# Freeing two kinds of PSUM bank earlier in the slot, and one matmul group moved by a slot, in a cross-attention and FFN kernel

## The chip, the cores and the metric

The kernel runs on one core of one Trainium2 chip. The metric is the device time of one execution in microseconds (us). A core has a matrix engine (PE; its weight loads are shown as PEld), a vector engine (DVE), an activation engine (ACT), a general engine (POOL) and a queue that starts transfers (SP). Each works through its own list of instructions in order, and they wait for each other with counting semaphores. PE writes only to PSUM, which has eight banks of 128x512 float32.

## The reference

```
x = x + attention(layernorm(x), ctx, mask)     # x 2x2048x512, ctx 2x128x512, 16 heads of 32
    q = layernorm(x) @ wq + bq ; k, v = ctx @ wk + bk, ctx @ wv + bv
    score = q k^T / sqrt(32) * mask ; where(score == 0, -1e9, score) ; softmax over the 128 keys
    out   = (softmax @ v) @ wo + bo
x = x + (real(ifft(fft(layernorm(x)) @ w_complex)) + bias)
```
The second part is linear, so the kernel folds the two Fourier transforms and the complex weights into one 512x512 matrix M in its first sixth, and then multiplies by M.

## The kernel before

The 4096 rows are cut into 16 chunks of 256 (chunk c). The heads of a chunk are worked in four groups of four, so there are 64 score tiles s = 4c + g (128 x 1024 scores each: two tiles of 128 rows, four heads, 128 keys). The main loop runs over slots v = 2 to 79; a chunk's worth of work is four slots, v = 4c + r with r = 0 to 3, and the stages are staggered over the slots:

- PE, slot v: every second slot (r even) the softmax-times-V product PV, from `weigh`; the transposes of score tile v-2 (`turn`, L606); one "mid" product (r = 0, 1: output projection WO of chunk c-2, half 0 or 1; r = 2, 3: FFN product FF of chunk c-3); the scores of tile v+1 (`scores`, L594); then the "late" products.
- DVE, slot v: scores times mask (`mask_mul`, L890), in odd slots the division of the context by the softmax sum (`ctx_norm`, L914), the replacement of zeros (`zero_to_neg`, L897), the row minimum (`least`, L902), then `lo(n)` for the held and the mid products, then layernorm statistics (`stats1`, `stats2`, L928, L971) and the reciprocal of the sums (`recip`, L908).
- ACT, slot v: in odd slots `copy_rec` (L725), four exponentials of tile v-1, two copies of transposed scores (L718), four more exponentials (L709), in odd slots `ctx_hi` (L732), then `hi(n)` for the held and the mid products, casts for the layernorms.
- POOL: the scale of the minimum into a bias for the exponentials (`bias`, L1124), low halves of split operands, bias additions, `spread` (L1131), which prepares R, and `stat_cols`, which prepares ST.

All products other than scores, transposes and PV are called fills and are numbered n in the order of PE's list. They share three PSUM banks: fill n goes to bank n mod 3 and may start only when fill n-3 is free. The kinds that matter are: QQ, a pair of query projections (24 matmuls, L454); R, the reciprocals turned by four transposes (L555); ST, the rows of layernorm statistics (two matmuls in `stat_rows`, L462); U and M, pieces of the folding of the FFN matrix; WO and FF (12 matmuls each, L449).

```
if n >= 3:
    pe.wait_ge(g_free, n - 2)
```
A bank is freed by DVE at the end of `lo(n)`, in the order of n. For QQ, DVE itself subtracts (L862) after ACT has made the high half (L683). For ST, ACT copies the rows (`stat_copy`, L649), and for R, ACT copies the bank in `copy_rec` (L725); DVE then only issues an empty instruction (L847) that adds one to `g_free`:

```
elif kind in ("ST", "R"):
    dve.engine_nop().then_inc(g_free, 1)
    return
```
Late fills of slot v are "held": their `hi` and `lo` run in slot v+1, behind `least` on DVE and behind the second four exponentials and `ctx_hi` on ACT. Mid fills are handled in their own slot. Before, the steady order of the fills is r0: WO, R, ST; r1: WO, QQ; r2: FF, R; r3: FF, QQ. That is nine fills for three banks, so each stands three places behind the same one in every chunk: QQ of r1 behind R of r0, FF of r2 behind ST, WO of r1 behind WO of r0.

Chunk c's queries and statistics go to their stacked form through 14 transfers on SP (`stack_q`, at slot 4c-5), of which the last two (`stack_rows`) wait for ST's copy.

Of the kernel before, what the change touches and what calls it, by code (L numbers as in the profile page):

```python
# [17 lines left out]
NC = NB * S // CH  # L18
# [18 lines left out]
def plan():  # L37

    fills, slots, held = [], {}, []
    lead = [("W1", 0), ("CT", 0), ("CT", 1), ("K", 0), ("ST", 0), ("Q", 0, 0), ("Q", 0, 1), ("S", 0),
            ("W1", 1), ("Q", 0, 2), ("S", 1), ("K", 1), ("Q", 0, 3), ("ST", 1), ("Q", 1, 0), ("S", 2),
            ("Q", 1, 1), ("Q", 1, 2), ("Q", 1, 3)]
    front = []
    for f in lead:
        if f[0] == "S":
            front += [("S", f[1], 0), ("S", f[1], 1)]  # L50
        else:
            front.append(("G", len(fills)))
            fills.append(f)
    early = {
# [3 lines left out]
    }  # L58
    queries = {2: (2, 0), 4: (2, 1), 5: (3, 0), 6: (3, 1)}
    for v in range(V0, V1):  # L60
        c, r = divmod(v, 4)
        mid = {
            0: [("WO", c - 2, 0)],
            1: [("WO", c - 2, 1)],
            2: [("FF", c - 3, 0)],
            3: [("FF", c - 3, 1)],
        }[r]
        mid = [f for f in mid if 0 <= f[1] < NC] + early.get(v, [])
        if mid == [LAST]:
            mid = [LAST, (*LAST, "right")]  # L70
        late = []
        if v % 2 == 0 and 0 <= v - 4 < NS:
            late.append(("R", (v - 4) // 2))
        if v % 4 == 0 and 3 <= v // 4 + 2 < NC:
            late.append(("ST", v // 4 + 2))
        if v in queries:
            late.append(("QQ",) + queries[v])
        elif v >= 7 and v % 2 == 1 and (v + 9) // 4 < NC:
            late.append(("QQ", (v + 9) // 4, (v + 9) % 4 // 2))
        base = len(fills)  # L80
        fills += mid + late
        mids = list(range(base, base + len(mid)))
        lates = list(range(base + len(mid), len(fills)))
        items = []
        if v % 2 == 0 and 0 <= v - 4 < NS:
            items += [("PV", (v - 4) // 2)]
        if 0 <= v - 2 < NS:
            items += [("PT", v - 2, 0), ("PT", v - 2, 1)]
        items += [("G", n) for n in mids]
        if 0 <= v + 1 < NS:  # L90
            items += [("S", v + 1, 0), ("S", v + 1, 1)]
        items += [("G", n) for n in lates]
        slots[v] = (items, held, mids)
        held = lates
    return fills, front, slots


def stats_slot(c, t):
# [7 lines left out]
def hi_slot(c):  # L106
    return 5 if c == 4 else 4 * (c - 3)
# [11 lines left out]
def build(nc, x, xt, ctx_in, mask, wq, bq, wk, bk, wv, bv, wo, bo, lparts, tables, bf, eye, sums, pick, places, heads, out):  # L119
    fills, front, slots = plan()  # L120
    at = {f: n for n, f in enumerate(fills)}

    with ExitStack() as stack:
# [519 lines left out]
        def _(act):  # L643
# [42 lines left out]
            def high_m(c):  # L686
                act.wait_ge(g_free, at["M", c] + 1)
                act.activation(mh[:, c, :], mf[:], ACT.Identity, scale=SO / D).then_inc(m_hi, 1)

            def split_hi(c):  # L690
                act.wait_ge(d_xt[c % NT], 16 * (c // NT + 1))
                if c >= 2:
                    act.wait_ge(g_done, last_query(c - 2) + 1)
                act.copy(xth[:, c % 2], xtr[:, c % NT]).then_inc(h1_done, 1)
# [8 lines left out]
            def exps(s, t):  # L703
                if t == 0:
                    act.wait_ge(p_nb, s + 1)
                for j in range(4):
                    z = zs[:, s % NZ, t, j, :]
                    i = 4 * t + j
                    last = act.activation(z, z, ACT.Exp, bias=nbias[:, s % 4, i:i + 1], scale=-NEG,  # L709
                                          accum_out=zsum[:, s % 4, i:i + 1])  # L710
                if t == 1:
                    last.then_inc(ex_done, 1)

            def copy_pt(s, f):
                act.wait_ge(pt_done, 2 * s + f + 1)
                if f == 0 and s >= 2:
                    act.wait_ge(pv_done, s // 2)
                act.copy(pt[:, s % 2, 2 * f:2 * f + 2, :], PB[f][:]).then_inc(pt_copied, 1)  # L718

            def copy_rec(m):  # L720
                n = at["R", m]
                act.wait_ge(g_done, n + 1)
                if m >= 1:
                    act.wait_ge(cn_done, m)
                act.copy(rec[:], G[n % 3][:].rearrange("p (i n) -> p i n", i=2)).then_inc(rc_done, 1)  # L725

            def ctx_hi(m):
                c, h = divmod(m, 2)
                act.wait_ge(cn_done, m + 1)
                if h == 0 and c >= 2:  # L730
                    act.wait_ge(g_done, at["WO", c - 2, 1] + 1)
                act.copy(ch[:, c % 2, 2 * h:2 * h + 2, :], cn[:]).then_inc(ch_done, 1)  # L732
# [37 lines left out]
            hi(at["Q", 1, 3])  # L770
            for v in range(V0, V1):
                c, r = divmod(v, 4)
                held, mids = slots[v][1:]
                if v % 2 == 1 and 0 <= v - 5 < NS:
                    copy_rec((v - 5) // 2)
                if 2 <= v - 1 < NS:
                    exps(v - 1, 0)
                if 0 <= v - 2 < NS:
                    copy_pt(v - 2, 0)
                    copy_pt(v - 2, 1)  # L780
                if v == 2:
                    act.wait_ge(d_wo, 16)
                    act.activation(wos[:], wos[:], ACT.Identity, scale=SO).then_inc(w_sc, 1)
                    act.wait_ge(w_sc, 1)
                    act.copy(woh[:], wos[:]).then_inc(w_hi, 1)
                if 2 <= v - 1 < NS:
                    exps(v - 1, 1)
                if v % 2 == 1 and 0 <= v - 5 < NS:
                    ctx_hi((v - 5) // 2)
                if 0 <= v - 9 < 4:  # L790
                    high_m(v - 9)
                for n in held:
                    hi(n)
                if v == 3:
                    split_hi(3)
                for n in mids:
                    hi(n)
                if r == 1 and 0 <= c - 2 < NC:
                    norm_hi2(c - 2, 0)
                if r == 2 and 0 <= c - 2 < NC:  # L800
                    norm_hi2(c - 2, 1)
                for a in range(4, NC):
                    if hi_slot(a) == v:
                        split_hi(a)
        @block.vector
        def _(dve):
# [103 lines left out]
            def ctx_norm(m):  # L910
                dve.wait_ge(rc_done, m + 1)
                if m >= 1:
                    dve.wait_ge(p_cl, m)
                dve.tensor_tensor(cn[:], CX[:].rearrange("p (i n) -> p i n", i=2), rec[:], ALU.mult).then_inc(cn_done, 1)  # L914
# [100 lines left out]
            lo(at["Q", 1, 3])  # L1015
            for v in range(V0, V1):
                c, r = divmod(v, 4)
                held, mids = slots[v][1:]
                if 0 <= v < NS:
                    mask_mul(v)  # L1020
                if v % 2 == 1 and 0 <= v - 5 < NS:
                    ctx_norm((v - 5) // 2)
                if 0 <= v < NS:
                    zero_to_neg(v)
                if 0 <= v < NS:
                    least(v)
                if 0 <= v - 9 < 4:
                    low_m(v - 9)
                for n in held + mids:
                    lo(n)  # L1030
                tasks = []
                tasks += [(stats1, mean1, a, t) for a in range(4, NC) for t in range(2) if stats_slot(a, t) == v]
                if r == 0 and 0 <= c - 2 < NC:
                    tasks.append((stats2, mean2, c - 2, 0))
                if r == 1 and 0 <= c - 2 < NC:
                    tasks.append((stats2, mean2, c - 2, 1))
                for stats, _, *ct in tasks:
                    stats(*ct)
                if v % 2 == 1 and 0 <= v - 3 < NS:
                    recip((v - 3) // 2)  # L1040
                for _, mean, *ct in tasks:
                    mean(*ct)
                if c - 2 == NC - 1 and r < 2:
                    last_lo2(r)
                if v in (4, 5):
                    for n in range(3 * v - 6, 3 * v - 3):
                        fold(n)
# [312 lines left out]
```

## Time and profile before

| | |
|---|---|
| median of three runs | 487.33 us (487.2 to 487.72) |
| profiled execution | 487.75 us, of which the span of its instructions is 486.0 us |
| PE busy | 441.3 us (91%) |
| DVE busy | 403.6 us (83%) |
| ACT busy | 366.8 us (75%) |
| POOL busy | 349.3 us (72%) |
| mean granted clock of PE | 0.993 of full speed |

Busy time says how long instructions of an engine were under way. Where two engines are both near the span, what matters is at which points one stands idle, and what ended that idle time. "DVEq" as a releaser is DVE's sequencer, here the empty instruction of L847.

### The profile page before, as it was taken

How to read it: one execution, taken by the hardware profiler on the slowest of the kernel's cores; microseconds unless marked ns; L12 is line 12 of the kernel's file. 1: busy time of each engine (PE TensorE's matmuls, PEld its weight loads, DVE VectorE, ACT ScalarE, POOL GpSimd, SP SyncE). 2: the span in 40 equal slices, each digit the busy share in tenths (PEclk: the TensorE clock that was granted, in tenths of full speed). 3: DMA queues.
4: the chain of work that ended last, by engine and by line, in shares of the span. 5: the costliest groups of instructions: out<-in, count | busy, mean ns of one | idle time of the engine just before them, and what ended most of it. 6: DMA issues, size and time to landing. Idle time of an engine off the chain costs nothing.

```text
span 486.0 us, 10923 instructions
## 1 busy us (share of the span) xinstructions
PE 441.3 (91%) x3510; PEld 298.5 (61%) x3510; DVE 403.6 (83%) x538; ACT 366.8 (75%) x1342; POOL 349.3 (72%) x476
## 2 busy tenths in 40 slices
PE   7989859968889898989898999989898989989897
PEld 5777647747566565656565656666565665655444
DVE  3797589867989898898989898989899888999543
ACT  3358757757978888878979888888888879989810
POOL 6579552853867969696969697887969776865663
PEclk9999999979999999999999999999999999999999
DMA  8995834223415355454445353535442333321334
GB/s 285 394 349 142 289 110 107 66 59 86 90 48 143 101 142 113 129 128 117 108 128 118 85 128 103 146 99 141 104 101 70 93 75 83 76 58 30 88 98 120
DMA packets 85286, 60.15 MB, mean 124 GB/s; under 512 B 40141, under 2 KB 72813, under 8 KB 84718
## 3 DMA queue, kind: packets, MB, share of 16 engines
q1 hardware_dynamic: 84508, 59.29, 45.5%
q8 instruction: 29, 0.48, 0.4%
q10 hardware_dynamic: 722, 0.17, 0.2%
q14 instruction: 27, 0.22, 0.1%
HBM read 29.33 MB, written 8.39 MB: 78 GB/s over the span
## 4 chain that ended last, share of the span: by engine, by line
PE 49%; DVE 24%; ACT 10%; issue 10%; DMA 3%; SPq 2%; POOL 1%; DVEq 0%; ACTq 0%; POOLq 0%
PE bank L454 16%; PE bank L449 16%; DVE zs L897 7%; ACT zs L709 6%; PE bank L606 6%; PE bank L620 5%; DVE nmin L902 4%; DVE zs L890 3%; DVE cn L914 2%; PE scores L594 2%; ACT pt L718 2%; DVE st L971 2%; DVE x L869 2%; SPq L287 2%; DMA cxs<-in_ctx 2%
## 5 line engine op out<-in xcount | busy, mean ns | idle before, releaser
L709 ACT ACTIVATE zs<-zs,nbias 128x128 f32<-128x128 f32 x512 | 199.5, 395 | 18.6 <-POOL nbias L1124 18.3
L718 ACT COPY pt<-bank 128x512 f32<-128x512 f32 x128 | 67.9, 581 | 41.5 <-PE bank L606 41.5
L709 ACT ACTIVATION_READ_ACCUMULATOR zs<-zs,nbias 128x1 f32 x512 | 98.5, 192 | 0.0
L897 DVE SCALAR_TENSOR_TENSOR zs<-zs 128x1024 f32<-128x1024 f32 x64 | 88.7, 1386 | 1.2
L902 DVE TENSOR_REDUCE nmin<-zs 128x8 f32<-128x1024 f32 x64 | 78.1, 1220 | 2.2
L454 PE MATMUL bank<-xth,wqh 128*128 128x256 f16 x224 | 61.5, 275 | 19.4 <-DVEq L847 16.6
L890 DVE TENSOR_TENSOR zs<-scores,ms 128x1024 f32<-128x1024 f32 x64 | 78.1, 1220 | 1.1 <-issue 0.6
L1084 POOL TENSOR_TENSOR xs<-xs,bob 128x512 f32<-128x512 f32 (+1 forms) x41 | 42.8, 1046 | 48.4 <-DVE zs L897 44.0
L606 PE MATMUL bank<-ident,zs 128*128 128x128 f32 x512 | 68.3, 276 | 1.9 <-ACT zs L709 1.9
L606 PEld LDWEIGHTS bank<-ident,zs 128*128 128x128 f32 x512 | 55.7, 140 | 15.3 <-issue 10.7
L454 PE MATMUL bank<-xth,wql 128*128 128x256 f16 x224 | 61.2, 273 | 0.0
L454 PE MATMUL bank<-xtl,wqh 128*128 128x256 f16 x224 | 61.2, 273 | 0.0
L449 PE MATMUL bank<-woh,ch 128*128 128x512 f16 x128 | 48.5, 379 | 2.9 <-POOL cl L1137 2.1
L449 PE MATMUL bank<-wol,ch 128*128 128x512 f16 x128 | 48.5, 379 | 0.0
L449 PE MATMUL bank<-woh,cl 128*128 128x512 f16 x128 | 48.5, 379 | 0.0
L449 PE MATMUL bank<-mh,x1h 128*128 128x512 f16 x120 | 45.5, 379 | 0.0
L449 PE MATMUL bank<-ml,x1h 128*128 128x512 f16 x120 | 45.5, 379 | 0.0
L449 PE MATMUL bank<-mh,x1l 128*128 128x512 f16 x120 | 45.5, 379 | 0.0
L1124 POOL TENSOR_SCALAR nbias<-nmin 128x8 f32<-128x8 f32 x64 | 15.8, 247 | 36.3 <-issue 18.9
L594 PEld LDWEIGHTS scores<-ks,qs 102*128 102x128 f16 (+1 forms) x480 | 32.1, 98 | 14.7 <-DVE zs L890 1.4
L1110 POOL TENSOR_TENSOR x<-x,bfb 128x512 f32<-128x512 f32 x32 | 40.7, 1274 | 0.0
L862 DVE TENSOR_TENSOR ql<-bank,qh 128x512 f16<-128x512 f32 x28 | 19.3, 691 | 25.4 <-ACT qh L683 24.3
(126 smaller groups left out, 950.6 us busy)
## 6 DMA issues: line engine op xcount, KB each, us to landing
xs<-in_x SPq DMA_DIRECT2D x16, 512.0 KB, 4.3
xtr<-in_xt SPq DMA_DIRECT2D x16, 512.0 KB, 4.5
out<-x SPq DMA_DIRECT2D x31, 256.0 KB, 2.5
qs<-qh SPq DMA_DIRECT2D x120, 64.0 KB
lp<-in_lparts SPq DMA_DIRECT2D x4, 1024.0 KB, 9.3
qs<-ql SPq DMA_DIRECT2D x60, 64.0 KB
ms<-in_mask SPq DMA_DIRECT2D x16, 128.0 KB, 2.5
wqs<-in_wq SPq DMA_DIRECT2D x2, 512.0 KB, 7.0
```

The lines of the kernel that those rows point to most:

```text
L449: last = pe.matmul(o, a, b, start=(i == 0), stop=(i == len(mm) - 1))
L454: last = pe.matmul(o, a, b, start=(first and i == 0), stop=(i == len(pairs) - 1))
L594: last = pe.matmul(A[:, n % 2, 128 * j:128 * j + 128], qs[c % 2][0:rows, g, j, 128 * t:128 * t + 128], ks[0:rows, g, j, c // (NC // NB), : ...
L606: last = pe.transpose(PB[f][:, a:a + 128], zs[:, s % NZ, t, 2 * f + i, :], ident[:])
L620: last = pe.matmul(CX[32 * j:32 * j + 32, 256 * i:256 * i + 256], vs[:, b, n:n + 32], pt[:, i, j, :], start=True, stop=True)
L709: last = act.activation(z, z, ACT.Exp, bias=nbias[:, s % 4, i:i + 1], scale=-NEG, accum_out=zsum[:, s % 4, i:i + 1])
L718: act.copy(pt[:, s % 2, 2 * f:2 * f + 2, :], PB[f][:]).then_inc(pt_copied, 1)
L890: dve.tensor_tensor(zs[:, s % NZ], A[:].rearrange("p t (h k) -> p t h k", h=4), ms[:, c % NM].unsqueeze(2).broadcast_to([128, 2, 4, KEYS]) ...
L897: dve.scalar_tensor_tensor(out=z, in0=z, scalar=0.0, in1=z, op0=ALU.is_equal, op1=ALU.subtract).then_inc(eq_done, 1)
L902: dve.tensor_reduce(nmin[:, s % 4, :], zs[:, s % NZ].rearrange("p t h k -> p (t h) k"), AX.X, ALU.min).then_inc(mn_done, 1)
L1084: i = pool.tensor_tensor(z, z, bob[:, n], ALU.add)
L1110: pool.tensor_tensor(z, z, bfb[:], ALU.add).then_inc(p_x1b, 1)
```

## The change

Held fills are split in two. R and ST of the slot before are now "prompt": ACT handles them right after `copy_rec`, ahead of its first exponentials, and DVE right after `ctx_norm` (after `mask_mul` in even slots), ahead of `zero_to_neg` and `least`. QQ stays where it was. In addition ST of chunk c moves from slot 4c-8 (r = 0, behind R) to slot 4c-9 (r = 3, ahead of QQ); chunk 3 goes from slot 4 to 3, chunk 4 from slot 8 to 10. The steady order becomes r0: WO, R; r1: WO, QQ; r2: FF, R; r3: FF, ST, QQ. No instruction is added or removed.

```diff
-        if v % 4 == 0 and 3 <= v // 4 + 2 < NC:
-            late.append(("ST", v // 4 + 2))
+        late += [("ST", a) for a in range(3, NC) if row_slot(a) == v]
...
-        slots[v] = (items, held, mids)
+        slots[v] = (items, [n for n in held if fills[n][0] in ("R", "ST")],
+                    [n for n in held if fills[n][0] not in ("R", "ST")], mids)
...
+def row_slot(c):
+
+    return {3: 3, 4: 10}.get(c, 4 * c - 9)
...
@@ ACT
-                held, mids = slots[v][1:]
+                prompt, held, mids = slots[v][1:]
                 if v % 2 == 1 and 0 <= v - 5 < NS:
                     copy_rec((v - 5) // 2)
+                for n in prompt:
+                    hi(n)
                 if 2 <= v - 1 < NS:
                     exps(v - 1, 0)
@@ DVE
-                held, mids = slots[v][1:]
+                prompt, held, mids = slots[v][1:]
                 if 0 <= v < NS:
                     mask_mul(v)
                 if v % 2 == 1 and 0 <= v - 5 < NS:
                     ctx_norm((v - 5) // 2)
+                for n in prompt:
+                    lo(n)
                 if 0 <= v < NS:
                     zero_to_neg(v)
```

## Rows read from the trace of the kernel before

**Rows 1.** One of the page's costliest groups: busy, mean ns of one, idle before and its releaser.
```profile
L454 PE MATMUL bank<-xth,wqh 128*128 128x256 f16 x224 | 61.5, 275 | 19.4 <-DVEq L847 16.6
```

**Rows 2.** Waits between 136 and 397 us: us in total, times, longest.
```profile
ACT pt L718 <- PE bank L606: 27.2, 20, 2.5
DVE ql L862 <- ACT qh L683: 17.4, 11, 2.0
...
PE bank L454 <- DVEq L847: 16.6, 11, 1.6
ACT zs L709 <- POOL nbias L1124: 11.0, 19, 1.1
...
DVE x L869 <- ACT srow L649: 4.5, 9, 0.6
...
PEld bank L462 <- DVE ql L862: 2.2, 10, 0.3
```

**Rows 3.** Stretches: us, then busy of PE, PEld, DVE, ACT, POOL; clock; DMA; GB/s.
```profile
240.12:266.14 26.02, 24.53 (x202) 16.35 (x202) 23.49 (x30) 21.96 (x83) 21.14 (x30) 1.00 0.51 129
...
97.00:111.00 14.00, 10.22 (x53) 7.03 (x51) 9.42 (x14) 7.81 (x32) 8.50 (x13) 0.76 0.19 52
404.00:456.00 52.00, 47.40 (x367) 28.32 (x366) 47.23 (x56) 48.27 (x194) 34.75 (x43) 1.00 0.32 70
```

**Rows 4.** DVE in order of time, one chunk (slots r1 to r0): start, us, instruction.
```profile
237.57 1.22 DVE L897 SCALAR_TENSOR_TENSOR zs<-zs 128x1024 f32<-128x1024 f32 x1
...
240.53 0.69 DVE L869 SCALAR_TENSOR_TENSOR x<-bank,xs 128x512 f32<-128x512 f32 x1 [0.49 <-ACT srow L649]
...
247.66 0.69 DVE L862 TENSOR_TENSOR ql<-bank,qh 128x512 f16<-128x512 f32 x1 [1.56 <-ACT qh L683]
...
250.89 0.68 DVE L914 TENSOR_TENSOR cn<-bank,rec 128x512 f32<-128x512 f32 x1
...
255.37 1.23 DVE L890 TENSOR_TENSOR zs<-scores,ms 128x1024 f32<-128x1024 f32 x1
```

**Rows 5.** The chain that ended last, from 238 to 267 us: start, us.
```profile
240.04 0.03 DVEq L847
...
252.34 2.62 PE bank L454 x24
```

**Rows 6.** PE in order of time, rows with idle time before them.
```profile
69.83 1.99 PE L454 MATMUL bank<-tb,lp 128*128 128x256 f32 x8 [3.22 <-DVEq L847]
...
103.45 3.78 PE L454 MATMUL bank<-tb,us 128*128 128x256 f32 x8 [3.78 <-DVEq L847]
...
130.09 0.29 PE L462 MATMUL bank<-ident,stok 128*128 128x128 f16 x2 [1.44 <-DVE ql L862]
...
135.80 0.28 PE L454 MATMUL bank<-xth,wqh 128*128 128x256 f16 x1 [1.50 <-DVEq L847]
...
396.23 0.28 PE L454 MATMUL bank<-xth,wqh 128*128 128x256 f16 x1 [1.49 <-DVEq L847]
```

**Rows 7.** DVE in order of time, rows with idle time before them.
```profile
72.27 0.76 DVE L827 TENSOR_TENSOR us<-bank,od 128x256 f32<-128x256 f32 x2 [1.47 <-ACT od L664]
...
79.63 0.69 DVE L862 TENSOR_TENSOR ql<-bank,qh 128x512 f16<-128x512 f32 x1 [0.52 <-ACT qh L683]
...
107.67 0.42 DVE L832 TENSOR_TENSOR mf<-bank,od 128x256 f32<-128x256 f32 x1 [3.68 <-ACT od L664]
...
115.93 0.69 DVE L881 SCALAR_TENSOR_TENSOR ml<-mf,mh 128x512 f16<-128x512 f32 x1 [3.02 <-ACT mh L688]
...
403.76 0.69 DVE L862 TENSOR_TENSOR ql<-bank,qh 128x512 f16<-128x512 f32 x1 [2.04 <-ACT qh L683]
```

**Rows 8.** One line's instructions: duration ns min/median/max.
```profile
L897 DVE SCALAR_TENSOR_TENSOR zs<-zs x64: 1212/1226/1986, 23.9 to 449.2; 128x1024 f32<-128x1024 f32 x64
```

**Rows 9.** ACT in order of time, around the turn from slot r3 to r0.
```profile
252.99 0.61 ACT L732 CAST ch<-cn 128x512 f16<-128x512 f32 x1
254.31 0.40 ACT L709 ACTIVATE zs<-zs,nbias 128x128 f32<-128x128 f32 x1 [0.71 <-POOL nbias L1124]
```

## The prediction

> **What bounds the kernel now.** I read the page's groups of instructions first, then the waits, then the stretches, and last the order of time of each engine over one chunk. In the groups, one of PE's lines stands out: the first matmul of a query projection follows 19.4 us of idle time, and 16.6 us of that ended at DVE's empty instruction of L847, which does nothing but free a bank [rows 1]. The waits of the steady part say the same: PE stopped 11 times for L847, 16.6 us together, DVE waited 11 times for QQ's high half (17.4 us) and 9 times for the copy of the statistics' rows (4.5 us); ACT, in turn, stood 27.2 us behind PE's transposes [rows 2], so it mostly follows PE.
>
> A chunk takes 26.02 us, and PE is busy in 24.53 of them at full clock, DVE in 23.49, ACT in 21.96, POOL in 21.14 [rows 3]. In order of time it is one loop: in slot r1 DVE runs `ctx_norm`, `zero_to_neg`, `least` and only then frees R [rows 4]; PE's projection starts right behind that (240.04 us, [rows 5]) and PE then works without a stop worth naming for the rest of the chunk. PE drags ACT, and ACT's high half of QQ drags DVE (1.56 us of waiting, [rows 4]), which comes late to free the next R. So the stop of 1.50 us is on the path, once a chunk, from 135.80 to 396.23 us: eleven stops, ten periods [rows 6].
>
> From 404 to 456 us DVE is busy in 47.23 us of 52 and ACT in 48.27 [rows 3]: there the two work at their own pace, and the whole tail starts when slot 53 lets it.
>
> **The change, part by part.** Nothing is added, so each part is a change of who waits.
>
> Freeing R behind `ctx_norm`. In r1 the bank comes free where `zero_to_neg` starts, 237.57, not at 240.04, some 2.4 us sooner [rows 4, 5]. PE's stop is 1.50, so it would vanish with 0.9 to spare. By itself this holds for every chunk.
>
> ST one slot earlier. It also turns the rotation: QQ of r1 now stands behind WO of r0, freed a slot before, WO of r0 behind FF of r3, FF of r2 behind R of r0, WO of r1 behind QQ of r3, QQ of r3 behind R of r2, R of r0 behind ST. I place each against the chunk shown, with PE 1.5 us earlier. The tightest is QQ of r3: R of r2 comes free when `ctx_norm` ends, 250.89 + 0.6 [rows 4] less the 1.5 by which DVE moves up as well, about 250.0; PE wants the bank at 252.34 - 1.5 + 0.1 for ST in front of it, about 250.9 [rows 5]. It fits with 0.9. WO of r0 has more than 2 us. So I cost the rotation at nothing in the steady part; if DVE fell 0.9 behind, PE would stop there instead. ST's own small wait for QQ (2.2 us over 10 chunks, [rows 2]) goes too, since ST is then behind FF of r2, long free.
>
> ACT's copy of ST at the head of r0. It lands between `ctx_hi`, which ends at 253.6, and the first exponentials, which waited 0.71 us for their bias [rows 9]; the copy needs less than that, so it is free. If the bias came 0.7 sooner it would cost 0.3. In r1 the copy is gone, and with it DVE's wait of 4.5/9 = 0.50 us [rows 2, 4].
>
> SP and POOL. `stack_rows` of chunk c waits for ST's copy; that copy is now earlier, except for chunk 4 (slot 11 in place of 9), where 12 transfers stand in front of it on SP. I count nothing.
>
> The steady period. PE needs 26.02 - 1.50 - 0.22 = 24.3 us for a chunk; DVE needs 26.02 - 17.4/11 - 4.5/9 = 23.9 [rows 2, 3]. ACT and POOL have more room, with 21.96 and 21.14 us of work a chunk [rows 3]. Nobody is far behind PE, so I don't take the whole of it: 24.3 is the floor, and I take 24.5, a gain of 1.5 a chunk. Over ten periods that is 15 us, 17 at the floor.
>
> What denser work costs is not in the trace. `zero_to_neg` takes 1.23 us in the median and up to 1.99 [rows 8]; if two of four a chunk rose from the one to the other, DVE would need 1.5 more, 25.4, and the gain were 0.6 a chunk. That is the other bound. The Trainium skill's page SBUF — State Buffer (Who interferes with whom) says that a DVE instruction with two SBUF inputs and a POOL instruction that reads SBUF share a port that only one of them holds at a time; this line has two such inputs, and its spread agrees. By that page the overlap would grow when idle time goes, which speaks for the second value.
>
> The front, up to slot 13. Its stops are larger, and the rotation differs there too. In slots 4 to 8 PE stops for 3.22 us before U of slot 5, behind R [rows 6]; after the change this U stands behind U of slot 4, freed a slot before. But DVE is at work without a pause in that slot and holds the next scores, so I count only the time that DVE waited behind: 1.47 there [rows 7], and about 1 in small waits around it, such as the 0.52 of slot 6 [rows 7]. That makes 2.5. In slot 9 PE stops for 3.78 us before M, again behind R [rows 6]; after, M stands behind M of slot 8, which has long been read. DVE waited 3.68 us for that M, and in the next slot 3.02 for its high half [rows 7]. With the stop gone both go, since the same projection and transposes come sooner by as much: 6.5 together. Part of that is clock: after the stop the eight matmuls took 3.78 us, against 1.99 for the eight of the U at 69.83, of the same shape [rows 6], and the granted clock over 97 to 111 us is 0.76 [rows 3], between the levels of 1.2 and 2.4 GHz. PE alone also loses the 1.44 before ST of slot 12 and the 1.50 of slot 13 [rows 6], about 2.5 that DVE doesn't gain at once. New in the front: the late ST of chunk 4 stands behind QQ of slot 9 and will stop PE by about 1.5, inside that lead. So the front gives DVE 9 us, PE 11.5. As bounds I take 5 (the later stops gone, the earlier ones turned into others) and 11.5.
>
> The end. DVE's last wait for QQ, 2.04 us at 403.76 [rows 7], lets it pick up PE's lead. So the tail starts earlier by something between DVE's sum and PE's: 9 + 15 = 24 and 11.5 + 15 = 26.5. I take 24.5. The tail itself has neither QQ nor ST, and its order of banks is the same in both kernels.
>
> Sum: the profiled execution took 487.75 us, its span 486.0, and 1.75 lies around it. 487.75 - 24.5 = 463.25. The runs' median is 0.4 below this execution, so 463.0 is the prediction. The far end is 11.5 + 17 = 28.5, so 459.
>
> **Rivals.**
> DVE becomes the bound. With `zero_to_neg` slower as above, a chunk takes 25.4 and the ten periods give 6; with 6 from the front and 1.5 of the last stop it is 13.5: 474. For it: DVE's need is only 0.4 under PE's. Against: its 23.9 already holds the slow cases of this chunk.
>
> The stops only move. A bank freed early lets PE reach the next wait (scores behind `mask_mul`, or QQ of r3 behind `ctx_norm`, which has 0.9 of room), and DVE, ACT and PE keep their spacing. Then only the 0.50 of DVE's wait a chunk and 2 of the front are won, 7 us: 480. The rule for it is in the Trainium skill's page TensorE: Matmul & The Clock Gate (A second HAM failure mode: psum-queue depth-cycling): small idles of PE between groups as it goes round its banks can lower its clock again and again. Here ten stops of 1.50 left the clock at 1.00 [rows 3], so the trace doesn't agree so far.
>
> Slower. DVE now waits for ACT's copy of ST ahead of `zero_to_neg` in r0, with `least`, the bias and the exponentials queued behind it. The copy can end at 253.9 [rows 9], and DVE reaches the wait at 255.37 + 1.2 = 256.6 [rows 4]: 2.7 us of room. It decides only if ACT fell 2.7 behind, and it eats the gain of 1.5 at 4.2; at 5 it would cost 0.8 in each of 12 chunks, and with the front's gain lost as well the time is 497. Nothing in the trace has ACT that late.
>
> No change at all: if the loop were set by something else, say the 1.50 is given back by ACT's chain of bias and exponentials. ACT waited for POOL only 11.0 us in these ten chunks [rows 2], and PE doesn't wait for it in r1, so I give it little.
>
> **How the numbers follow.** Forecast 0.68, its own range 459 to 469. DVE bound 0.17 (469 to 477). Stops move 0.08 (477 to 486). No change 0.03. Slower 0.04. The range 459 to 475 leaves out some 0.2. A time within 0.2% is about what a measurement of this kernel can't tell from no change: faster 0.93, same 0.03, slower 0.04.
>
> **What the profile after would show.** PE's waits for L847 gone or near it; the chunk at 24.3 to 24.8 us between first matmuls of the r1 projection; DVE's wait for the high half under 0.5 a chunk; the M of slot 9 in 2.0 us with the clock at 1.00 around 100 us; `zero_to_neg` with a mean still near 1.4. What would make me wrong: a mean above 1.6 there, a new stop of PE before the r3 projection or the scores, or DVE idle before `zero_to_neg` in r0.

## The result, and the profile after

The changed kernel takes 457.39 us in the median (457.07 to 457.88, four runs), the kernel before, run beside it, 487.29: a ratio of 0.9386, 95% interval 0.9369 to 0.9402. That is 29.9 us. The prediction said 463.0 and 459 to 475: right in sign and mechanism, but the kernel is 5.6 us faster than that, and the time lies 1.6 us below the range. The profiled execution took 457.07 us, its span is 455.3, against 487.75 and 486.0.

The stretches of the changed kernel (us, then busy of PE, PEld, DVE, ACT, POOL; clock; DMA; GB/s) answer to [rows 3]: one chunk from QQ of slot r1 to the next, and the stretch in the front in which PE's clock had fallen.
```profile
292.99:317.18 24.19, 24.19 (x206) 16.39 (x204) 23.46 (x31) 22.10 (x84) 21.42 (x30) 1.00 0.53 133
...
97.00:111.00 14.00, 12.36 (x112) 10.17 (x111) 13.09 (x20) 12.36 (x46) 10.67 (x11) 1.00 0.17 49
```
A chunk takes 24.19 us in place of 26.02, and PE is busy in all of it. From 97 to 111 us the granted clock is 1.00, not 0.76.

The page's groups, with the mean ns of one and the idle time before, against [rows 1] and [rows 8] (all lines have moved by five or more):
```profile
L904 DVE SCALAR_TENSOR_TENSOR zs<-zs 128x1024 f32<-128x1024 f32 x64 | 90.3, 1411 | 1.2
...
L723 ACT COPY pt<-bank 128x512 f32<-128x512 f32 x128 | 67.8, 580 | 14.3 <-PE bank L611 13.9
...
L459 PE MATMUL bank<-xth,wqh 128*128 128x256 f16 x224 | 61.1, 273 | 1.3 <-DVE ql L869 1.3
```
The 19.4 us before QQ are 1.3. `zero_to_neg` costs 1411 ns on average, 25 ns more than before (1386 then). The M of slot 9 takes 1.89 us, not 3.78.

The waits from 111 to 370 us answer to [rows 2]:
```profile
ACT zs L714 <- POOL nbias L1133: 11.5, 28, 0.8
...
ACT pt L723 <- PE bank L611: 7.0, 11, 1.2
...
DVE ql L869 <- ACT qh L688: 2.8, 7, 1.4
```
No wait of PE for the empty instruction is left. ACT's wait for PE fell from 27.2 to 7.0 us, DVE's for the high half from 17.4 to 2.8: the engines that followed PE no longer do so by much.

The chain that ended last, over the same chunk, is now this (start, us):
```profile
293.15 2.62 PE bank L459 x24
295.77 1.00 PE bank L625 x16
296.77 1.02 PE bank L611 x8
297.79 2.59 PE bank L454 x12
300.38 0.45 PE scores L599 x8
300.83 0.44 PE bank L560 x4
301.27 0.87 PE bank L611 x8
302.15 2.59 PE bank L454 x12
304.74 0.45 PE scores L599 x8
305.19 0.11 PE bank L467 x2
305.30 2.62 PE bank L459 x24
```
It is PE alone, back to back. Before, it went round through ACT, DVE and the empty instruction once a chunk. These are lines of the chain of the kernel before, from behind those of [rows 5] to the next empty instruction:
```profile
255.96 0.60 PE bank L606 x4
...
256.58 0.57 ACT pt L718 x2
...
257.54 1.65 ACT zs L709 x8
259.19 0.48 ACT qh L683
...
263.68 1.14 DVE zs L897
...
264.84 1.22 DVE nmin L902
266.06 0.04 DVEq L847
```

What PE still waits for ahead of the tail, in order of time:
```profile
72.92 1.97 PE L459 MATMUL bank<-tb,lp 128*128 128x256 f32 x8 [1.38 <-issue]
77.12 0.28 PE L459 MATMUL bank<-xth,wqh 128*128 128x256 f16 x1 [1.34 <-DVE ql L869]
...
107.37 0.28 PE L467 MATMUL bank<-ident,stok 128*128 128x128 f16 x2 [1.65 <-DVE ql L869]
...
120.48 0.39 PE L454 MATMUL bank<-woh,ch 128*128 128x512 f16 x1 [0.57 <-DVE ql L869]
```
The third is the stop that the prediction named, the late ST of chunk 4 behind QQ of slot 9 (1.5 forecast, 1.65 found). The 3.22 before U of slot 5, the 3.78 before M of slot 9, the 1.44 of slot 12 and the 1.50 of slot 13 [rows 6] are gone.

Where the time came from can be read off the starts of QQ, since PE carries the path. PE starts QQ of slot 13 at 123.63 us in place of 135.80, which is 12.17 earlier, and QQ of slot 53 at 365.56 in place of 396.23, which is 30.67 earlier. So the front gave 12.2, the ten steady periods 18.5. The spans differ by 30.7, so what the tail gives and takes comes to nothing.

### The profile page after: what moved, and what is told of

Same layout as the page of the kernel before. It is cut to its first block, busy times and chain, and to the rows that moved or that the text cites. A ratio compares the mean times of both kernels' runs of the same rounds, so it can differ in the third digit from the quotient of the medians.

```text
span 455.3 us, 10923 instructions
## 1 busy us (share of the span) xinstructions
PE 434.1 (95%) x3510; PEld 296.9 (65%) x3510; DVE 403.8 (89%) x538; ACT 368.2 (81%) x1342; POOL 353.1 (78%) x476
## 4 chain that ended last, share of the span: by engine, by line
PE 69%; DVE 14%; issue 5%; ACT 5%; DMA 3%; SPq 2%; POOL 1%; ACTq 1%; DVEq 0%; POOLq 0%
PE bank L454 30%; PE bank L459 15%; PE bank L611 9%; PE bank L625 5%; PE scores L599 4%; DVE zs L904 4%; ACT zs L714 3%; DVE zs L897 3%; PE bank L560 2%; SPq L292 2%; DMA xs<-in_x 1%; PE bank L541 1%; DMA bqb<-in_bq 1%; DVE x L882 1%; DVE st L935 1%
## 5 line engine op out<-in xcount | busy, mean ns | idle before, releaser
L904 DVE SCALAR_TENSOR_TENSOR zs<-zs 128x1024 f32<-128x1024 f32 x64 | 90.3, 1411 | 1.2
L1146 POOL TENSOR_TENSOR cl<-cn,ch 128x512 f16<-128x512 f32 x32 | 37.7, 1177 | 3.9 <-ACT ch L737 3.9
```

Of the source, the lines that this page charges most:

```text
L904: dve.scalar_tensor_tensor(out=z, in0=z, scalar=0.0, in1=z, op0=ALU.is_equal, op1=ALU.subtract).then_inc(eq_done, 1)
L1146: pool.tensor_tensor(cl[:, c % 2, 2 * h:2 * h + 2, :], cn[:], ch[:, c % 2, 2 * h:2 * h + 2, :], ALU.subtract).then_inc(p_cl, 1)
```

## The experiments

Each was run beside the kernel before, whose medians there were 487.8 to 489.1 us. Its time goes with the granted clock: of its 30 executions, two with a mean clock of 0.996 took 484.7 and 484.9 us, 13 with 0.993 took 486.5 to 488.7, and 15 with 0.989 or 0.990 took 488.8 to 490.0. The changed kernel's were all at 0.999 or 1.00. So small differences are read from the traces, and the clock is named where it differs. A second set of the changed kernel gave the measure of repetition:

> The changed kernel once more, on the chip of the run beside it, as a measure for comparisons between calls: 457 to 458 us; by the theory 3 to 5 us under the run beside it.

457.45 us (457.08 to 457.78), ratio 0.9368, 0.9343 to 0.9393. It repeats to 0.1 us; the run beside it (r_signal, below) is 4.8 us slower, as expected.

### Which half of the edit does it

**Early freeing alone.** ST stays where it was.
```diff
-        late += [("ST", a) for a in range(3, NC) if row_slot(a) == v]
+        if v % 4 == 0 and 3 <= v // 4 + 2 < NC:
+            late.append(("ST", v // 4 + 2))
```


> The early freeing alone: R and ST are prompt as in the changed kernel, ST stays in its old slots (4c-8), so the rotation is the old one. Theory (the stop in r1 was a wait for DVE's place in its list, and PE is the bound once it is gone): R is free when ctx_norm ends, before PE asks; a small stop of 0.2 to 0.4 us stays before ST in r0, behind QQ of r3. A chunk takes 24.3 to 24.6 us, the whole 457 to 462 us. Rival (the gain is the turned rotation, which puts no fill behind a late R): the stop in r1 stays near 1.5, 480 to 487 us.

461.12 us, ratio 0.9459 (0.9415 to 0.9502): two executions at a clock of 1.00 took 459.8 and 460.4, two at 0.996 461.8 and 462.2. In its trace a chunk takes 24.35 us, 1.67 less than before, and no stop for the empty instruction is left between 125 and 370 us. What remains is the small stop before ST, seen in the waits of that stretch:
```profile
PEld bank L468 <- DVE ql L870: 2.3, 10, 0.3
```
At slot 53 it is 3.4 us behind the changed kernel, of which 1.7 arose by slot 13 and 0.16 more in each period. The theory's numbers hold; the rotation isn't needed for the big stop, and it is worth 0.16 us a chunk.

**Moved ST alone.** The new slots, everything freed behind `least`.
```diff
-        slots[v] = (items, [n for n in held if fills[n][0] in ("R", "ST")],
-                    [n for n in held if fills[n][0] not in ("R", "ST")], mids)
+        slots[v] = (items, [], held, mids)
```


> The moved ST alone: new slots of ST and so the new rotation, but R and ST freed behind least as before. Theory: the stop moves from r1 to r3, where QQ now stands behind R of r2, freed behind least of r3; a chunk takes 25.5 to 26.0 us, and only the front's stops go (10 to 12 us): 474 to 479 us. Rival (rotation is what helps): 24.2 to 24.5 us a chunk, 457 to 462 us.

481.3 us, ratio 0.9886 (0.9834 to 0.9939). The stop has moved, as the theory said, from r1 to r3, where QQ now stands behind R of r2. PE in order of time, rows with idle time before them:
```profile
109.56 0.28 PE L466 MATMUL bank<-ident,stok 128*128 128x128 f16 x2 [1.49 <-DVE ql L868]
115.81 0.28 PE L466 MATMUL bank<-ident,stok 128*128 128x128 f16 x2 [2.90 <-DVEq L853]
...
299.18 0.28 PE L458 MATMUL bank<-xth,wqh 128*128 128x256 f16 x1 [1.67 <-DVEq L853]
325.21 0.28 PE L458 MATMUL bank<-xth,wqh 128*128 128x256 f16 x1 [1.67 <-DVEq L853]
```
325.21 - 299.18 is 26.03 us a chunk: nothing is won in the steady part. The front won 7.1 us (at QQ of slot 13), not the 10 to 12 that I expected. The first row is no loss, since the changed kernel has that stop too (1.65). Against the changed kernel 2.3 us are missing at QQ of slot 9 (100.63 in place of 98.30), which stands behind the late R of slot 8 and waits 1.72 us for the empty instruction, and 5.2 at QQ of slot 11, behind the 2.90 of the second row. That, and in two of the four executions a clock of 0.996 or 0.993 (481.9 and 483.2 us, against 480.0 and 480.7 at 1.00), is why the median lies 2 us over the expected range.

**One signal alone.** The smallest form: the kernel before, with R's empty instruction moved behind `ctx_norm`.
```diff
                     ctx_norm((v - 5) // 2)
+                for n in held:
+                    if fills[n][0] == "R":
+                        lo(n)
...
                 for n in held + mids:
-                    lo(n)
+                    if fills[n][0] != "R":
+                        lo(n)
```


> The kernel before with one thing moved: DVE's empty instruction that frees R's bank stands behind ctx_norm instead of behind least. ST, its copy and the rotation are as before. Theory (the stop in r1 is all there is to the steady part): the period falls to 24.35 as with the early freeing of both, the front gets a little less: 460 to 463 us. Rival (ST's copy at the end of r1 on ACT, behind which DVE waited 0.50 us a chunk, holds the loop once R is early): 24.8 us a chunk or more, 464 to 470 us.

462.27 us, ratio 0.9463 (0.9432 to 0.9494). A chunk takes 24.35 us (starts of QQ 323.53 and 347.88), so the rival is out: once R is early, ST's late copy on ACT holds nothing. Most of the gain hangs on an instruction that does no work and stood behind some 2.5 us of work that had nothing to do with it.

**ST held, R prompt, new slots.**
```diff
-        slots[v] = (items, [n for n in held if fills[n][0] in ("R", "ST")],
-                    [n for n in held if fills[n][0] not in ("R", "ST")], mids)
+        slots[v] = (items, [n for n in held if fills[n][0] == "R"],
+                    [n for n in held if fills[n][0] != "R"], mids)
```


> The changed kernel, but only R is prompt; ST is copied and freed behind the exponentials and least of r0 as before, in its new slots. Theory (what matters is R's bank): R of r0 stands behind this ST, and in the changed kernel PE asks for it some 0.4 us after least of r0 has ended, so it just fits: 457 to 459 us. Rival (ST's early copy carries part of the gain): a stop of 0.5 to 1.5 us before R of r0 in each of 11 chunks, 463 to 475 us.

461.61 us, ratio 0.9448 (0.942 to 0.9476), 2.6 above the expected range; 1.2 of that goes with the clock, since the execution at 1.00 took 460.38 and the three at 0.996 took 461.5 to 462.2. In the steady part the theory is right to the last digit: 24.19 us a chunk (320.46 to 344.65), and R of r0 isn't stopped there (only once ahead of it, in slot 12, by 0.49). The loss is in the front, 3.2 us at QQ of slot 13 (126.81), at a place that I hadn't looked at: QQ of slot 11 stands behind the ST of slot 10.
```profile
107.81 0.28 PE L467 MATMUL bank<-ident,stok 128*128 128x128 f16 x2 [1.65 <-DVE ql L869]
114.05 0.28 PE L459 MATMUL bank<-xth,wqh 128*128 128x256 f16 x1 [2.71 <-DVEq L854]
```
So ST's early freeing pays in the front alone, where the ST of slot 10 stands three fills ahead of the QQ of slot 11.

### Do front and steady part add?

**The change up to slot 13 only.** Prompt fills before slot 13 and ST of chunks 3 to 5 moved; the old rule for the rest.
```diff
+        late += [("ST", a) for a in range(3, 6) if row_slot(a) == v]
+        if v % 4 == 0 and 6 <= v // 4 + 2 < NC:
+            late.append(("ST", v // 4 + 2))
...
+        slots[v] = (items, [n for n in held if fills[n][0] in ("R", "ST") and v < 13],
+                    [n for n in held if fills[n][0] not in ("R", "ST") or v >= 13], mids)
```


> The change only up to slot 13 (prompt fills before slot 13, ST of chunks 3 to 5 moved), the old order after it. Theory (front and steady part add): the first old stop comes back in slot 17, DVE is then some 11.7 us early as in the changed kernel, and nothing more is won: 26.02 us a chunk after that, 475 to 477 us in all. Rival (the front's lead is absorbed later, the whole gain is the period): 483 to 487 us.

476.19 us, ratio 0.9755 (0.970 to 0.981). PE's lead is 11.71 us at QQ of slot 13 and 11.41 at slots 17 to 53, without a change of more than 0.02, with the old stop of 1.50 back in every chunk. The parts add: 11.4 for the front, the rest for the period. (The changed kernel's 12.17 at slot 13 is 0.46 more, a difference that is there already at the QQ of slot 5, 66.72 us against 67.20.)

### What bounds it now

**More work for PE.** Nine matmuls more in each of 11 chunks.
```diff
+                        if f == 1 and i == 0 and c >= 5:
+                            for _ in range(9):
+                                pe.matmul(o[:, 0:256], mm[0][0], mm[0][1], start=True, stop=True)
                         last = full_mm(o[:, 256 * i:256 * i + 256], mm)
```


> The changed kernel with nine more matmuls of 128x256 at the head of the second QQ of chunks 5 to 15 (their result is overwritten by the same group): about 0.98 us more work on PE in each of 11 chunks. Theory (PE is the bound over the whole steady part, without slack): each chunk longer by 0.98, 468.2 us in all (467 to 469). Rival (DVE or ACT is the bound and PE has slack): 457 to 462 us.

468.74 us (468.31 to 468.94), ratio 0.9603 (0.9558 to 0.9648). A chunk takes 25.17 us (325.96 to 351.13), 0.98 more; the nine take exactly that. PE in order of time:
```profile
351.13 1.15 PE L556 MATMUL bank<-xth,wqh 128*128 128x256 f16 x9
352.11 0.27 PE L459 MATMUL bank<-xth,wqh 128*128 128x256 f16 x1
```
Eleven times 0.98 is 10.8 of the 11.3 us between the medians; the rest is there before the first QQ of the main loop (its loads landed 0.4 later). PE has no slack at all.

**More work for DVE.** The scratch result isn't read.
```diff
+                if t == 0 and 3 <= c <= 13:
+                    for i in range(2):
+                        dve.bn_stats(stx[:, i, :], x1[:, n % NO, :])
                 dve.bn_stats(st2[:, t, :], x1[:, n % NO, :]).then_inc(s2_done, 1)
```


> The changed kernel with two more statistics instructions on DVE (0.6 us each, start to start, their result is not used) in one slot of each of 11 chunks, 1.2 to 1.3 us more work a chunk. Theory (PE is the bound, but DVE's need of 23.9 us a chunk is only 0.3 below the 24.19 measured): the period rises by what is over, 0.9 to 1.0, 467 to 469 us. Rival (DVE has real slack, since its busy time is 23.46 us of 24.19): 457 to 463 us, with DVE's waits taking it up.

466.42 us (466.31 to 466.62), ratio 0.9557 (0.9513 to 0.9602), between the two. DVE in order of time shows what was added, 343.68 to 344.88:
```profile
343.68 1.29 DVE L981 BATCH_NORM_STATS2 stx<-x 128x6 f32<-128x512 f32 x2
344.88 0.68 DVE L982 BATCH_NORM_STATS2 st<-x 128x6 f32<-128x512 f32 x1
```
1.20 us a chunk were added, and the chunk grew to 24.88 (322.56 to 347.44), by 0.69. PE stops again, once a chunk, this time for the scores behind `mask_mul`:
```profile
322.10 0.62 PE L600 MATMUL scores<-ks,qs 102*128 102x128 f16 x8 [0.52 <-DVE zs L898]
346.98 0.62 PE L600 MATMUL scores<-ks,qs 102*128 102x128 f16 x8 [0.52 <-DVE zs L898]
```
The chain that ended last runs over DVE's own list from 322 us to these scores. So by this difference DVE needs 24.88 - 1.20 = 23.7 us for a chunk, not 23.9, and has 0.5 of slack. The rival "DVE becomes the bound" was real, but half a microsecond away.

### Is a stop in the front on the path?

**ST of chunk 4 in slot 8.**
```diff
-    return {3: 3, 4: 10}.get(c, 4 * c - 9)
+    return {3: 3, 4: 8}.get(c, 4 * c - 9)
```


> The changed kernel with ST of chunk 4 back in slot 8 (it is in slot 10, where PE stops 1.65 us for its bank). Theory (each stop of PE before the tail is on the path, since PE's lead is carried to the end): 455.7 to 456.2 us. Rival (DVE limits at that place, and the tail starts by DVE): no change, 457.2 to 457.6.

457.08 us (456.89 to 457.29), ratio 0.9359 (0.9333 to 0.9384). Its median is 0.3 below the changed kernel's two sets, from other chips; its span is 455.2 against 455.3. I take it as no change, so my theory fell. The 1.65 is gone, but PE stops for others in its place:
```profile
107.68 0.70 PE L459 MATMUL bank<-tb,us 128*128 128x256 f32 x2 [0.93 <-DVE ql L869]
110.31 0.62 PE L599 MATMUL scores<-ks,qs 102*128 102x128 f16 x8 [0.64 <-DVE zs L897]
```
0.93 + 0.64 is 1.57, nearly the old 1.65. QQ of slot 13 starts at 123.60 us, as in the changed kernel (123.63). In slots 9 to 12 DVE sets the pace, and a stop of PE there is only the place at which it waits. From slot 13 on PE's work is on the path, as pe_plus shows.

## Why the prediction was right and wrong

**Right.** The stop of r1 was DVE's place in its list, R is free before PE asks, PE becomes the bound; r_signal and prompt_alone show it. The rotation costs nothing in the steady part; the tight place that I named, QQ of r3 behind `ctx_norm` (0.9 forecast), has 0.5 of room in the changed kernel: `ctx_norm` of that slot ends at 256.27, where the next instruction starts, and QQ starts at 256.75. The copy of ST on ACT costs nothing. SP and POOL don't show. The clock came back with the stop of slot 9 gone. The smaller and the slower rivals didn't come; slots_alone shows what "the stops only move" looks like, and that it takes a bank still freed behind `least`.

The rule that I put beside the rival of the moved stops is another matter. The Trainium skill's page TensorE: Matmul & The Clock Gate (A second HAM failure mode: psum-queue depth-cycling) speaks of small idles of PE that cost clock, not of stops that only move. In the traces the clock is 1.00 with the stops of 1.50 us, with the 1.67 of slots_alone and without any, so no trace here shows that cost for idles of this size.

**Wrong: the steady period, by 3.5 us of the 6.2 missed in the span.** The step that failed is "PE needs 26.02 - 1.50 - 0.22 = 24.3 us for a chunk" and "so I don't take the whole of it: 24.3 is the floor, and I take 24.5". Both halves of it failed. First, the stop is larger than its printed idle time. The profile counts idle time from the modelled end of the last matmul, which lies behind the moment at which the next could have been issued: in the changed kernel eight score matmuls show 0.61 us in the timeline and 0.45 in the chain, and it is the 0.45 after which QQ starts. So the stop printed as 1.50 was worth 1.66. The weight loads, whose list stood idle before the same QQ, say it directly (waits of the kernel before, 136 to 397 us: 1.68 each):
```profile
PEld bank L454 <- DVEq L847: 16.8, 10, 1.8
```
prompt_alone measured 1.67 a chunk for this stop alone, and 0.16 is left for ST's small one, which I had at 0.22: 1.83 together, as found (26.02 - 24.19). Second, the margin of 0.2, taken because nobody is far behind PE, had no row behind it. PE had nothing to share, and DVE's 1 us more in ten chunks (`zero_to_neg` 1386 to 1411 ns, forty times) fell into its slack. Ten periods gave 18.5 (1.83 each, and 0.2 once, where a stop of before was longer), not 15.

**Wrong: what reaches the end, 2.0 us.** I put the tail's start "between DVE's sum and PE's" and took 24.5 of 24 to 26.5. It was PE's sum: DVE's lead is 28.7 us at `least` of slot 54 (371.80 us, before 400.50) and 30.7 at that of slot 55 (377.35, before 408.01). Between the two lies QQ's low half, which before waited 2.04 us for the high half [rows 7] and now starts with no idle time printed before it:
```profile
371.80 1.22 DVE L909 TENSOR_REDUCE nmin<-zs 128x8 f32<-128x1024 f32 x1
373.09 0.69 DVE L869 TENSOR_TENSOR ql<-bank,qh 128x512 f16<-128x512 f32 x1
```
At slot 53 DVE (28.7) is still behind PE (30.7), and one wait later it has caught up. ACT and DVE had the room to follow PE, which I had in the rows ([rows 3], busy 21.96 and 23.49 of 26.02) and didn't use.

**The front, 0.7 us short.** 11.5 forecast for PE, 12.2 found; 9 for DVE, 9.6 found (`least` of slot 13 at 124.89 in place of 134.50). The terms were 2.5, 6.5 and 2.5. PE's lead is 3.26 at the QQ of slot 7, 9.57 at that of slot 9 and 12.17 at that of slot 13, so they measured 3.3, 6.3 and 2.6. The first term was the one sized too small.

The range was too short below for the same reasons. Its far end, 11.5 + 17, was meant as the case with nothing lost, but 17 held the undersized stop; with 18.3 and 12.2 it would have been 457. The rest is small: 463.25 less 0.4 is 462.85, which I put down as 463.0.

**The port.** The Trainium skill's page SBUF — State Buffer (Who interferes with whom) made me weigh a slower `zero_to_neg`. The instruction reached 2.05 us in the changed kernel (1.99 before) and rose by 25 ns on average, against the 380 that the rival needed. The rule may name the cause of the spread, which no run here tests; overlap in a period shorter by 7% didn't bring much more of it.

**Open: what part of the gain is the clock.** In the trace of the kernel before the clock stood at its lower level from 102 to 108 us, from the second half of PE's stop in slot 9 on:
```profile
104.00:106.00 2.00, 2.00 (x6) 1.60 (x5) 0.00 (x0) 0.00 (x0) 1.71 (x2) 0.50 0.00 0
106.00:108.00 2.00, 2.00 (x12) 1.54 (x12) 0.33 (x1) 0.73 (x2) 0.00 (x0) 0.50 0.00 0
```
No run separates the stop from the clock, but the executions of one kernel at different clocks bound it. From 0.993 to 0.996 the kernel before gains 2.5 us (middle times 487.3 and 484.8), and from 0.989 to 0.993 2.0; prompt_alone gains 1.9 from 0.996 to 1.00. Two such steps lead from 0.993 to 1.00, so my estimate is that 4 to 5 of the 29.9 us are clock. The low clock isn't bound to the stop of slot 9 either: the profiled execution of r_signal (mean clock 0.996) has no stop before that M, and its clock is 0.50 from 64 to 66 us, just behind the 2.00 us for which PE stands before the QQ at 62.76. The kernel before has the same 2.00 at 62.95, with a clock of 1.00 from 60 to 70 us.

## What to carry to other kernels

Look for signals that stand behind work they don't depend on: here an empty instruction, 2.5 us too late in its engine's list, cost a stop on the path in each of 11 chunks, and moving it alone gave 25.6 us, against 29.9 for the whole change. When one engine will be the bound, add up its own pieces in the chain, issue to issue, over one period (here 24.17 of 24.19 us), and take that for the new period in place of the old one less the printed idle times. A stop in a stretch where another engine sets the pace is worth nothing by itself; ask which engine's lead survives to the end.

## What the runs showed that I hadn't expected

The two engines are very even: DVE needs 23.7 us a chunk, PE 24.19, and between them the coupling costs under 0.02 us. I had thought that two engines within 2% of each other, which hand buffers back and forth several times a chunk, would lose some tenths to each other; pe_plus shows 0.98 for 0.98 and the changed kernel PE busy in 24.19 of 24.19.
